# A grouped convolution and a per-sample mix on one core: the eight samples of a unit in plain order

## The reference

```python
# x: (128, 64, 1024), cond: (128, 128)
y = x + conv1d(x, weight, padding=4, taps=9, groups=4)          # 64 -> 64 channels
      + (cond @ c_weight.T)[:, :, None] + fside[None, :, None]
h = gelu(gelu(cond @ W0 + b0) @ W1 + b1)
att = softmax(h @ W2 + b2)                                      # (128, 8), per sample
agg_w = einsum('bk,koi->boi', att, weight_k)                    # a 64x64 matrix per sample
out = y + einsum('boi,bih->boh', agg_w, y) + (att @ bias_k)[:, :, None]
```

## Time and profile before

| | |
|---|---|
| median of 3 runs | 261.31 us (260.1 to 261.76) |
| the profiled execution | 261.07 us |
| its span in the trace | 258.6 us |
| TensorE busy | 241.1 us, 93% |
| VectorE busy | 225.9 us, 87% |
| ScalarE busy | 88.1 us, 34% |
| moved by DMA | 68.77 MB, mean 266 GB/s |

### The profile page before, as it was taken

The page is one execution under the profiler, slowest core; times in us unless marked ns, Lnnn a source line. Parts: engine busy times, 40 slices in busy tenths (PEclk is TensorE's granted clock), DMA queues, the critical chain, the costliest instruction groups (busy, mean ns, idle before and its releaser), DMA issues.

```text
span 258.6 us, 5721 instructions
## 1 busy us (share of the span) xinstructions
PE 241.1 (93%) x2144; PEld 112.5 (44%) x2144; DVE 225.9 (87%) x146; ACT 88.1 (34%) x142; POOL 25.1 (10%) x48
## 2 busy tenths in 40 slices
PE   2579989999999999999999999999999999999980
PEld 1322323344444444444444455555555555554520
DVE  1350599999999999999999999999999999999871
ACT  2352301233333334241414333333334142333091
POOL 0010152010101001010101010100101010101000
PEclk9999999999999999999999999999999999999998
DMA  7999619999999999999999999999999998544078
GB/s 229 313 253 207 146 38 223 272 214 313 278 260 344 227 381 249 369 252 331 298 314 285 294 325 290 330 250 370 261 361 246 329 301 294 215 162 165 0 309 340
DMA packets 29337, 68.77 MB, mean 266 GB/s; under 512 B 3264, under 2 KB 5312, under 8 KB 29328
## 3 DMA queue, kind: packets, MB, share of 16 engines
q1 hardware_dynamic: 19392, 51.31, 63.0%
q10 hardware_dynamic: 9936, 17.34, 28.5%
HBM read 35.08 MB, written 33.55 MB: 265 GB/s over the span
## 4 chain that ended last, share of the span: by engine, by line
PE 80%; issue 7%; DVE 6%; ACT 2%; DMA 2%; ACTq 0%; POOLq 0%; DVEq 0%; POOL 0%
PE yps L475 56%; PE zps L495 18%; PE zps L458 3%; DVE ycol L372 2%; DVE xph L364 2%; DMA mlps<-in_mlp 2%; DVE ynat L381 1%; ACT mixt L291 1%; PE zps L522 1%; PE yps L522 1%; ACT zout L283 1%; ACT L312 0%; PE zps L562 0%; POOLq L44 0%; ACTq L306 0%
## 5 line engine op out<-in xcount | busy, mean ns | idle before, releaser
L475 PE MATMUL yps<-xph,wraw 64*64 64x512 f32 x1488 | 169.9, 595 | 1.3 <-DVE xph L364 1.1
L283 ACT ACTIVATE zout<-zps,gamu 128x512 f32<-128x512 f32 x120 | 72.8, 688 | 136.6 <-PE zps L495 117.0
L475 PEld LDWEIGHTS yps<-xph,wraw 64*64 64x64 f32 x1488 | 76.7, 133 | 88.5 <-issue 88.4
L372 DVE STREAM_TRANSPOSE ycol<-yps 128x1024 f32<-128x1024 f32 x62 | 75.7, 1227 | 13.7 <-PE yps L475 12.6
L364 DVE STREAM_TRANSPOSE xph<-xin 128x2112 f32<-128x2112 f32 x32 | 74.7, 2337 | 0.0
L381 DVE STREAM_TRANSPOSE ynat<-ycol 128x2048 f32<-128x2048 f32 x30 | 67.6, 2290 | 1.1
L495 PE MATMUL zps<-ynat,mixv 64*64 64x512 f32 x480 | 61.4, 609 | 0.7 <-ACT zout L283 0.6
L495 PEld LDWEIGHTS zps<-ynat,mixv 64*64 64x64 f32 x480 | 24.6, 132 | 28.8 <-issue 28.7
L228 POOL COPY mixv<-mixt 128x512 f32 (+1 forms) x16 | 17.6, 1099 | 176.9 <-ACT zout L283 176.9
L291 ACT ACTIVATE mixt<-zps 128x1024 f32<-128x1024 f32 x8 | 7.8, 1021 | 11.7 <-PE zps L458 11.7
L458 PE MATMUL zps<-zout 32*128 32x512 f32 x32 | 9.2, 1011 | 2.2 <-ACT mixt L291 1.3
(11 more groups left out here) (47 smaller groups left out, 30.4 us busy)
## 6 DMA issues: line engine op xcount, KB each, us to landing
out<-zout SPq DMA_DIRECT2D x60, 512.0 KB, 9.6
xin<-in_x SPq DMA_DIRECT2D x60, 258.0 KB, 9.1
xin<-in_x ACTq DMA_DIRECT2D x60, 258.0 KB, 8.5
out<-xin SPq DMA_DIRECT2D x4, 512.0 KB, 4.3
xin<-in_x ACTq DMA_DIRECT2D x4, 132.0 KB, 5.8
xin<-in_x SPq DMA_DIRECT2D x4, 130.0 KB, 5.8
xin<-in_x SPq DMA_DIRECT2D x4, 128.0 KB, 6.2
xin<-in_x ACTq DMA_DIRECT2D x4, 126.0 KB, 6.2
```

The source lines that it names most:

```text
L283: nc.scalar.activation(zout[:, o].rearrange("p (i c j q) -> p c i j q", i=2, c=2, q=PH)[:, c], zps[:, at:at + BANK].rearrange("p (q i j) - ...
L372: nc.vector.transpose(ycol[:, :, :, :, :, g].rearrange("p i s j q c -> p i (s j) q c"), yps[:, 2 * BANK * (g % 2):2 * BANK * (g % 2) + 2 * ...
L475: last = nc.tensor.matmul(yps[C * c:C * c + C, at:at + BANK].rearrange("p (s f) -> p s f", s=S // 2), wsum[rows, b, g], xph[slot][c][rows, ...
```

## The change

The 8 samples of a unit are no longer split in two. Wherever samples lie side by side they now stand in plain order, and position runs innermost in `xph` and `ynat`. What follows from this in the code:

- `phases` writes `xph` as [group][sample][position]. The 32 words of a block, which are (sample, group), go to 32 places, each 66 words (next sample) or 528 words (next group) from another. Before, each two words, the two values of `t`, went to neighbouring places.
- `y_natural` still writes runs of 32 words. `conv` reads 8 runs of 64 words instead of 4 runs of 128. `mix` reads 8 runs of 64 neighbouring words, where it read 512 words with a step of two.
- A load covers 32 neighbouring partitions, where two loads covered 16 partitions each with a step of two. There are half as many, each with twice the bytes. ACT's queue takes the half i = 1 first, SP's still i = 0.
- In front, conv(0, 0) follows the first aggregation, and the others stand between the convolutions of unit 0. ACT issues its part of load 2 after the second aggregation's gathers instead of after all.
- In the last unit the pairs of samples are mixed in the order 0, 1, 2, 3 instead of 0, 2, 1, 3.

```diff
-        xph = [[sb(f"xph{i}{c}", [P, G, S // 2, NJ + 2, 2]) for c in range(2)] for i in range(2)]
-
-        ycol = sb("ycol", [P, 2, S // 2, NJ // 16, PH, G, 8])
-
-        ynat = [sb(f"ynat{i}", [P, S // 2, PH, 2, NJ, 2]) for i in range(2)]
+        xph = [[sb(f"xph{i}{c}", [P, G, S, NJ + 2]) for c in range(2)] for i in range(2)]
+
+        ycol = sb("ycol", [P, 2, S, NJ // 32, PH, G, 8])
+
+        ynat = [sb(f"ynat{i}", [P, PH, 2, S, NJ]) for i in range(2)]
...
-        def x_places(slot, i, k, t, at, n):
-
-            first = C * i + 32 * k + t
-            return xin[slot][first:C * i + 32 * k + 32:2][:, :, at - H * i + PAD:at - H * i + PAD + n]
+        def x_places(slot, i, k, at, n):
+
+            first = C * i + 32 * k
+            return xin[slot][first:first + 32][:, :, at - H * i + PAD:at - H * i + PAD + n]
...
                 for i in range(2):
-                    for t in range(2):
-                        sp.dma_start(*x_piece(slot, u, i, 0, t)).then_inc(x_in[slot], 16)
+                    sp.dma_start(*x_piece(slot, u, i, 0)).then_inc(x_in[slot], 16)
...
-                for i in range(2):
-                    for t in range(2):
-                        act.dma_start(*x_piece(slot, u, i, 1, t)).then_inc(x_in[slot], 16)
+                for i in (1, 0):
+                    act.dma_start(*x_piece(slot, u, i, 1)).then_inc(x_in[slot], 16)
...
                 nc.vector.transpose(
-                    xph[slot][c][:].rearrange("q g s j t -> q j s g t"),
+                    xph[slot][c][:].rearrange("q g s j -> q j s g"),
                     xin[slot][:, :, Q * c:Q * c + Q + 2 * PH].rearrange("q c (j p) -> q j c p", p=PH)).then_inc(turned, 1)
...
                 nc.vector.transpose(
-                    ynat[slot][:, :, :, i].rearrange("p s q (j i) t -> p s j q (i t)", i=16),
+                    ynat[slot][:, :, i].rearrange("p q s (j i) -> p (s j) q i", i=32),
                     ycol[:, i].rearrange("p s j q g c -> p (s j q g c)")).then_inc(ynat_made, 1)
...
-                                xph[slot][c][rows, g, :, b:b + NJ].rearrange("p s j t -> p s (j t)"),
+                                xph[slot][c][rows, g, :, b:b + NJ],
...
-                            ynat[slot][rows, 2 * (o % 2) + s, :, :, :, o // 2].rearrange("p q i j -> p (q i j)"),
+                            ynat[slot][rows, :, :, 2 * o + s].rearrange("p q i j -> p (q i) j"),
...
             aggregate(0)
-            aggregate(1)
-            aggregate(2)
             pe.wait_ge(w_sum, 1)
             conv(0, 0, 0)
+            aggregate(1)
+            conv(0, 0, 1)
+            aggregate(2)
+            conv(0, 0, 2)
             aggregate(3)
-            conv(0, 0, 1)
+            conv(0, 0, 3)
```

More of the change, by code:

```diff
@@ L159, in z_last @@
         def z_last(o):
-            return (yps, zps)[o % 2][:, 2 * BANK * (o // 2):2 * BANK * (o // 2) + 2 * BANK].rearrange(
+            return (yps, zps)[o // 2][:, 2 * BANK * (o % 2):2 * BANK * (o % 2) + 2 * BANK].rearrange(
                 "p (c f) -> p c f", c=2)
@@ L187, in _ @@
             for k in range(KQ):
-                for t in range(2):
-                    sp.dma_start(*x_piece(0, 0, 0, k, t, 0)).then_inc(x_first, 16)
+                sp.dma_start(*x_piece(0, 0, 0, k, 0)).then_inc(x_first, 16)
             for k in range(KQ):
-                for t in range(2):
-                    sp.dma_start(*x_piece(0, 0, 0, k, t, 1)).then_inc(x_in[0], 16)
+                sp.dma_start(*x_piece(0, 0, 0, k, 1)).then_inc(x_in[0], 16)
             sp.dma_start(consts, const_w).then_inc(const_in, 16)
@@ L212, in _ @@
                     store(u, o)
-            for n, o in enumerate(last_pairs):
-                sp.wait_ge(z_act, n + 1)
-                sp.wait_ge(z_dve, n + 1)
+            for o in range(PR):
+                sp.wait_ge(z_act, o + 1)
+                sp.wait_ge(z_dve, o + 1)
                 sp.dma_start(z_rows(NU - 1, o), out_last(o)).then_inc(z_out[o], 16)
@@ L304, in _ @@
             nc.scalar.activation(h1, sps[:, 0:NS], ACT.Gelu, bias=b0s).then_inc(act_mlp, 1)
-            for t in range(2):
-                act.dma_start(*x_piece(0, 0, 1, 1, t, 1)).then_inc(x_in[0], 16)
+            act.dma_start(*x_piece(0, 0, 1, 1, 1)).then_inc(x_in[0], 16)
             act.wait_ge(mm, 2)
@@ L317, in _ @@
                 gather(a, 1)
-            load(2, 0)
+                if a == 1:
+                    load(2, 0)
             act.wait_ge(const_mm, 1)
@@ L339, in _ @@
             act.wait_ge(turned, 2 * NU - 2)
-            for n, o in enumerate(last_pairs):
-                act.wait_ge(last_mixes, n + 1)
+            for o in range(PR):
+                act.wait_ge(last_mixes, o + 1)
                 nc.scalar.activation(
@@ L441, in _ @@
                     nc.vector.transpose(
-                        ynat[1][:, 2 * sh:2 * sh + 2, :, i].rearrange("p s q (j i) t -> p s j q (i t)", i=16),
-                        ycol[:, i, 2 * sh:2 * sh + 2].rearrange("p s j q g c -> p (s j q g c)")).then_inc(last_nat, 1)
+                        ynat[1][:, :, i, 4 * sh:4 * sh + 4].rearrange("p q s (j i) -> p (s j) q i", i=32),
+                        ycol[:, i, 4 * sh:4 * sh + 4].rearrange("p s j q g c -> p (s j q g c)")).then_inc(last_nat, 1)
             dve.wait_ge(gam_cut, NU)
-            for n, o in enumerate(last_pairs):
-                dve.wait_ge(last_mixes, n + 1)
+            for o in range(PR):
+                dve.wait_ge(last_mixes, o + 1)
                 nc.vector.tensor_scalar(
@@ L522, in mix_last @@
                         last = nc.tensor.matmul(
-                            z_last(o)[C * s:C * s + C, c], mixv[1][rows, 2 * o + s],
-                            ynat[1][rows, 2 * (o % 2) + s, :, :, :, o // 2].rearrange("p q i j -> p (q i j)"),
+                            z_last(o)[C * s:C * s + C, c].rearrange("p (q j) -> p q j", j=NJ), mixv[1][rows, 2 * o + s],
+                            ynat[1][rows, :, :, 2 * o + s].rearrange("p q i j -> p (q i) j"),
                             start=True, stop=True)
@@ L591, in _ @@
             pe.wait_ge(last_cols, 4)
-            for o in last_pairs:
-                pe.wait_ge(last_nat, 2 * (o % 2) + 2)
-                if o % 2 == 1:
-                    pe.wait_ge(z_made, 8 * NU - 10 + 2 * (o // 2))
+            for o in range(PR):
+                pe.wait_ge(last_nat, 2 * (o // 2) + 2)
+                if o >= 2:
+                    pe.wait_ge(z_made, 8 * NU - 14 + 2 * o)
                 mix_last(o)
```

36 lines of the change are left out of this document (15 added, 21 removed).

## The result

The changed kernel takes **298.09 us** (median of 4 runs, 297.15 to 298.77) against 261.31 us for the kernel before beside it (median of 3 runs; a fourth, of 326.33 us, fell into a slower state and is not counted). The ratio is **1.143** (95% interval 1.139 to 1.147; the two medians alone give 1.141). The profiled execution took 297.54 us and has a span of 295.7 us. Forecast were 297 us and a span of 294.2.

The account below looks back on a forecast made before the run. TensorE at 13.92 us a unit, VectorE at 13.80; slower phases make VectorE's unit 16.46. Span 258.6 - 0.3 (start) + 35.9 (14 units) = 294.2, with 2.5 around it 297 us; range 283 to 314 us.

Parts of the forecast that it names:

- The tie: Steady unit: TensorE sets 13.92 us and VectorE needs 13.80 of them, so added VectorE work lengthens the unit.
- The phases: VectorE's transposed write to xph: 1.7 ns a lone word, 3.59 us an instruction, 1.33 us more each, 2.66 per unit.
- POOL's copy: POOL's copy stepping through mixt in SBUF, 1099 ns or 2.15 ns a word, read as evidence near the ceiling.
- The ceiling: Rival on the phases' write: 2.14 ns a word or more, a unit of 18.3 us, about 327 us; chance 0.03.
- The sum: Whole run: unit 16.46 us, 35.9 us more over 14 units, start 0.3 us earlier, span 294.2, time 297 us.
- The mix: TensorE's mix reads without the step: 0.02 us less a round, 0.16 us a unit, counted at nothing.
- the convolution's reads from an odd word: TensorE's convolution at tap b = 1: no row shows a cost, at most 0.16 us a unit, counted at nothing.
- Loads and queues: DMA loads: half as many with twice the bytes, SP and ACT at different halves; worth nothing.
- Free lone words: Rival on the phases' write: lone words cost nothing extra, VectorE stays at 13.80 us a unit, 257 us; chance 0.11.
- a small cost: Rival on the phases' write: 0.12 to 0.18 ns more a word, 264 to 267 us; chance 0.05.
- A slowed TensorE: Rival in the steady part: TensorE slows because it now waits, giving a unit above 27 us; chance 0.01.
- the start on its own: Start, within the no-cost rival: first convolution at 16.2 instead of 21.1 us, saving 0 to 4.9, say 3 us.

Follow-up runs that it names:

- pair-of-groups kernel: Changed kernel with xph keeping pairs of neighbouring channel groups, so phases writes two words and convolution reads with a step of two; 267.03 us, ratio 1.020.
- the changed layout with shorter hops: Changed kernel with xph laid out as [sample][group][position], lone words hopping 66 words throughout instead of mostly 528; 309.32 us, ratio 1.184.

## Why the prediction was right

**What bounds the kernel.** The tie of 13.92 and 13.80 us a unit was read rightly. The pair-of-groups kernel shows it from the other side: as soon as TensorE has 14.4 us to do, it sets the pace and VectorE waits for it (0.5 us a unit ahead of y_columns).

**The phases.** This term carried the forecast: 3.59 us each expected, 3.63 to 3.64 measured, 1.72 ns a word for the 1.7 taken. It was the least certain: the rows left 1.07 to 2.14 open, and I chose in the upper half from POOL's copy and from the view that the port works in pairs. So far as the rows go, that the choice came within 0.02 was luck. POOL's copy could not carry it: POOL's multiplication in SBUF, which reads and writes neighbouring words, takes 1046 ns for 512 words in the same trace against the copy's 1099. It has a second input and so is no exact twin, but the copy's 2.15 ns a word need not come from its hops at all:

```profile
L249 POOL TENSOR_TENSOR zout<-zout,expv 128x512 f32<-128x512 f32 x1 | 1.0, 1046 | 16.5 <-ACT zout L320 16.5
```

The Trainium skill's 1.71 ns (Vector Engine (DVE) Microarchitecture Reference, 5.2) hit it within 0.01, and the runs show that its rule covers a transpose. Pairs of groups, at 2338 ns, show that it is the number of words side by side that counts, from an even word. The ceiling, a lone word as long as a pair, was not reached by hops of 66 words either (1.87 ns). My picture behind it, a port that visits one 8-byte place at a time, does not explain 1.36 ns for straddling pairs.

**The sum.** Per unit 16.46 forecast, 16.49 measured; unit 1 at 42.6, measured 42.45; the first y_columns near 23.7, measured 23.33. Of the start, 0.3 us is chance: the first convolution took 4.46 us where I had 4.8 (1.7 times what the next one takes, not twice), and over the traces above it ranges from 3.91 to 5.35. The span came out 1.5 us longer than the sum: 0.2 us lies before y_columns 0 of unit 15 (273.25 against 273.0), the rest behind it, 22.4 us where I took the old 21.2. Timeline of the end, changed kernel:

```profile
286.52 3.74 SPq L210 DMA_DIRECT2D out<-xin  x4
...
287.23 1.61 DVE L438 TENSOR_SCALAR xin<-zps,gamu 128x512 f32<-128x512 f32 x2
```

VectorE is done at 288.8, and 6.9 us pass to the end of the span; before, 5.4 us. The last stores land later, 5.7 us from issue in the median instead of 4.3:

```profile
out<-xin SPq DMA_DIRECT2D x4, 512.0 KB, 5.7
```

Nothing shows that this is the change's doing. The kernel before with the new start, profiled twice, has 21.2 us from that same point to its end in one profile and 22.6 in the other, and the changed layout with shorter hops has 21.2. Both lengths occur with either layout. That the time itself, 298.09, came within 1.1 us of 297 owes something to a second small miss the other way: 1.8 us lie around the span of the profiled execution, not 2.5.

**The mix.** Its mean fell from 609 to 594 ns, and its rounds from 0.450 to 0.430 us in the kernel with pairs of groups, where the same mixes follow without a gap, as expected (0.02 each). It was right to count it at nothing, since TensorE waits. That the convolution's reads from an odd word are free was my assumption at a bound of 0.16 us a unit; the mean is 597 ns against 595, no cost that shows.

**Loads and queues.** Counted at nothing, and nothing by the kernel that changes ACT's queue alone (259.06 against 259.11 us). The transfers themselves did change: stores land in 4.3 us in the median instead of 9.6. A longer unit with less traffic at a time is not needed for that: the change in ACT's queue alone does most of it, on the kernel before with the new start at an unchanged pace; first without, then with it:

```profile
out<-zout SPq DMA_DIRECT2D x60, 512.0 KB, 9.5
...
out<-zout SPq DMA_DIRECT2D x60, 512.0 KB, 5.2
```

Loads land in 7.4 and 7.5 us there instead of 9.0 and 8.4. The rival of that experiment was right that the transfers get faster, and wrong that the time follows: no engine had waited for them.

**The rivals.** Free lone words, a small cost and the ceiling fall with the phases' 3757 ns. A slowed TensorE falls with a granted clock of 1.00 between 100 and 150 us and with convolutions that take as long as before (597 against 595 ns in the mean), although it stands idle for 18% of the span. Its price was misread as well. The slow first convolution does not show what waiting costs: in the kernel before it follows on work without a gap and took 4.80 us at a granted clock of 1.00, in the changed kernel it comes after 5.1 us of idle time and took 4.46. And by that row (4.8 against 2.8) a slowed unit would be 23.6 us, not 27. For the start on its own I had put 3 us with a span of 0 to 4.9; on the kernel before it brought 2, since 1.8 of it went into waiting for POOL's chain to the bias.

## What to carry to other kernels

Before changing a layout, list who writes and who reads each buffer, and for each the run of neighbouring words: a lone float32 in SBUF cost 1.7 to 1.9 ns on VectorE's write and 1.7 ns on TensorE's read, a word of a pair on an even word 1.07 ns on VectorE's write. If a hop can't be avoided, pair whatever dimension lies innermost (samples or groups did it equally), put it on the side that touches each word least often, and prefer the engine with time to spare. The last is advice and was not tried by itself. Two engines within 1% of each other mean that a change to either must be costed on both.

## What I had not expected

- A pair that straddles an even boundary costs 1.36 ns a word on VectorE's write, between the aligned pair (1.07) and the lone word (1.72).
- Lone words 66 apart cost 1.87 ns each, mostly 528 apart 1.72.
- TensorE's moving read costs 0.430 us a round of 512 words in runs of 64 or 128, 0.450 to 0.457 with a step of two words, and 0.875 with a step of 32.
- Turning round the order of ACT's loads (with load 2 issued earlier) brought the landing of the stores from 9.5 to 5.2 us, with no effect on the time.
- The first convolution took from 3.91 to 5.35 us in these traces, 0.9 us apart in two profiles of one kernel.
